# First conv of a graph-network kernel by three half-rate products, with its weight sums and the blend moved in the opening

## The chip, the cores and the metric

One NeuronCore of a Trainium2 chip runs the whole kernel. The metric is the device time of one execution in microseconds (us). The engines are named as in the profile: PE is TensorE, DVE is VectorE, ACT is ScalarE, POOL is GpSimd, SP only starts DMAs.

## What is computed

For 64 graphs of 128 nodes with 128 features, x and a 0/1 adjacency:

```
h = relu(layernorm(x))
c = relu(bn1(conv1(h)))                       # kernel width 1
x_conv = relu(bn2(conv2(c)) + h)              # width 17, padded by 8, along the nodes
s = h @ w_se.T + b_se                         # 3 coordinates
A = exp(-|s_n - s_m|^2) * adj
x_nmp = A @ relu(h @ w_msg.T + b_msg)
GRU gates r, z, n from [x_conv, x_nmp] and h; y = (1-z)*n + z*h
x = x + y
x = x + adj @ (relu(layernorm(x)) @ weight) + bias
```

## The kernel before

The graphs are worked on in 16 groups of four, and the groups in pairs: one pair (eight graphs) is a conv pass. `opening()` on every engine handles the first pair and prepares the second; then `step(t)`, t = 1 to 7 (the last without a front), runs the conv of pair t, the gates of that pair, the second layer of the pair before it and the front (norm, conv1, messages, distances) of the pair after. There is no scheduler: each engine's program is written out by hand, and semaphores (`have`, `wait_ge`, `then_inc`) tie the engines together. An engine works strictly in its written order.

Every product of 32-bit operands is split: each operand is rounded to a short part (`_hi`, by ACT's copy) and a rest (`_lo`, by DVE's subtraction), and `split_product` does three matmuls, hi x hi, hi x lo, lo x hi, of 512 or 256 columns.

The width-17 conv holds the nodes in four phases (node index modulo 4), `c1[:, 0:4]`. From `step(1)` on it is done by nine products of a quarter of the length over sums and differences of phases (`px`, made by `pre` on POOL) and over sums of taps (`conv` parts `M12`, `M22`, `M21`). For the first pair the kernel before uses the plain form instead: `direct(tap)` for 17 taps, each into both banks, pQ for the even outputs and pP for the odd ones. It then needs no differences, and POOL forms the tap sums (`sum_phases`) for `step(1)` meanwhile.

Names that the change touches, by engine:

- PE: `direct`, `x_turn(g)` (transposes of normed rows into PSUM), `rows_turn`, `distances`, `neighbour_sums`, `messages`, `gates_h`, `gates_n`, `gates_c`, `o_turn` (turns the blended output back), `keep_clock` (matmuls without use).
- ACT: `round_w(k)` rounds part k of the conv weights, `split_hi` and `split_hi_phases` round conv inputs to `cx_hi`, `conv1_out` writes `c1`, `first(g)` applies the norm, `hidden(g)` writes h, `left_rows`, `decay` (exp), `conv_round`, and the gates' tanh.
- DVE: `split_w(k)`, `split_lo` (`cx_lo`), `normalise1` (statistics), `shift1` (`nb`), `conv_out`, `conv_lo_out` (`xc_lo`), `sums_lo` (`n_lo`), `blend_start` and `blend_end` (the GRU blend), `residual`.
- POOL: `scale1` (the power -1/2 of the variance, `rs`), `pre`, `sum_phases`.

`f_done[i]` tell ACT and DVE that a conv product is complete. In the opening `f_done[3]` releases `conv_out(0, 0)` and `f_done[4]` releases `conv_out(0, 1)`. `residual(0)` follows the blend of group 0, and `messages(5)` is the messages product of group 5, in the front of `step(1)`.

## Time and profile before

| | us |
|---|---|
| median of three runs | 346.11 |
| lowest and highest | 343.37, 346.34 |
| the profiled execution, its own time | 344.95 |
| its span in the profile | 342.6 |
| TensorE busy in the span | 329.8 |
| VectorE busy | 261.6 |
| ScalarE busy | 220.5 |
| GpSimd busy | 152.1 |

The mean granted clock of TensorE was 0.995 of full speed. The profile shows one execution. The span runs from the first to the last instruction; the profiled execution's own time is 2.35 us longer, for what lies around it. In a timeline a row gives start, duration, engine, line, operation and tiles, and in brackets how long the engine had been idle before and what ended that. A matmul's duration includes filling and draining the array, so that matmuls in a row overlap; what each costs is the distance between two starts.

### The profile page before, as it was taken

To read this page: it belongs to the slowest core of one execution; us is meant where nothing else is said; L and a number is where in the kernel's file an instruction comes from. 1 tells how busy PE (TensorE), PEld (TensorE's weight loads), DVE (VectorE), ACT (ScalarE), POOL (GpSimd) and SP (SyncE) were. 2 spreads that over 40 slices of the span, in tenths; PEclk is the share of its full clock that TensorE was granted. 3 is DMA by queue.
4 is the path that set the end of the run, shared out by engine and by line. 5 is a ranking of instruction groups with operands and counts; after the bars stand their busy time and mean duration, and the time that the engine had idled before them with its cause. 6 is when DMAs were issued, how large, how long until landed. Compare 5 with 4: busy or idle time off the path is not lost.

```text
span 342.6 us, 6310 instructions
## 1 busy us (share of the span) xinstructions
PE 329.8 (96%) x2198; PEld 296.3 (86%) x2198; DVE 261.6 (76%) x735; ACT 220.5 (64%) x431; POOL 152.1 (44%) x131
## 2 busy tenths in 40 slices
PE   7699979999999999999999999999999999999995
PEld 5489958799988999899988999889988998899894
DVE  5576896899688995899688995899687895784474
ACT  2938835876865876676865876676866763444353
POOL 7053271024952189024952189024950189029014
PEclk9989999999999999999999999999999999999999
DMA  7900020001220022001210023001100000000003
GB/s 234 340 5 0 6 89 0 2 1 33 92 64 0 2 83 76 29 0 33 94 62 0 2 71 114 2 0 33 64 32 2 0 33 31 2 1 2 0 1 123
DMA packets 7951, 15.02 MB, mean 44 GB/s; under 512 B 1008, under 2 KB 1648, under 8 KB 7792
## 3 DMA queue, kind: packets, MB, share of 16 engines
q1 hardware_dynamic: 7776, 14.62, 12.7%
q8 instruction: 17, 0.28, 0.4%
q14 instruction: 14, 0.11, 0.1%
q10 hardware_dynamic: 144, 0.01, 0.0%
HBM read 10.43 MB, written 4.19 MB: 43 GB/s over the span
## 4 chain that ended last, share of the span: by engine, by line
PE 65%; DVE 19%; ACT 9%; issue 4%; POOL 1%; DMA 1%; POOLq 0%; DVEq 0%; ACTq 0%
PE pQ L311 4%; PE pQ L312 4%; PE pQ L313 4%; PE pNR L311 4%; PE pNR L313 4%; PE pNR L312 4%; PE pF L424 4%; PE pP L311 4%; PE pP L312 4%; PE pP L313 4%; DVE st L981 3%; ACT work L750 2%; PE pZ L484 2%; PE pI L313 2%; PE pI L311 2%
## 5 line engine op out<-in xcount | busy, mean ns | idle before, releaser
L1331 POOL TENSOR_TENSOR rs<-ve,neg_half 128x4 f32<-128x4 f32 x15 | 15.6, 1040 | 90.6 <-DVE ve L1111 90.6
L1326 POOL TENSOR_TENSOR rs<-ve,neg_half 128x8 f32<-128x8 f32 (+1 forms) x9 | 15.5, 1721 | 73.1 <-DVE ve L988 73.1
L311 PE MATMUL pP<-cx_hi,conv_hi 128*128 128x256 f32 x154 | 45.0, 292 | 0.0
L313 PE MATMUL pP<-cx_hi,conv_lo 128*128 128x256 f32 x154 | 43.5, 282 | 0.0
L312 PE MATMUL pP<-cx_lo,conv_hi 128*128 128x256 f32 x154 | 43.3, 281 | 0.0
L311 PE MATMUL pQ<-cx_hi,conv_hi 128*128 128x256 f32 x126 | 37.0, 293 | 0.0
L750 ACT ACTIVATE work<-work,nb,rs 128x128 f32<-128x128 f32 x60 | 24.8, 483 | 17.5 <-DVE nb L1115 17.0
L312 PE MATMUL pQ<-cx_lo,conv_hi 128*128 128x256 f32 x126 | 35.4, 281 | 0.0
L313 PE MATMUL pQ<-cx_hi,conv_lo 128*128 128x256 f32 x126 | 35.3, 281 | 0.0
L311 PEld LDWEIGHTS pP<-cx_hi,conv_hi 128*128 128x128 f32 x154 | 29.1, 189 | 0.3
L312 PEld LDWEIGHTS pP<-cx_lo,conv_hi 128*128 128x128 f32 x154 | 29.1, 189 | 0.3
L313 PEld LDWEIGHTS pP<-cx_hi,conv_lo 128*128 128x128 f32 x154 | 29.0, 188 | 0.0
L1069 DVE TENSOR_TENSOR cx_lo<-px,cx_hi 128x576 fp32r<-128x576 f32 x28 | 27.2, 1008 | 0.8 <-ACT cx_hi L664 0.8
L312 PEld LDWEIGHTS pQ<-cx_lo,conv_hi 128*128 128x128 f32 x126 | 23.8, 189 | 0.3
L311 PEld LDWEIGHTS pQ<-cx_hi,conv_hi 128*128 128x128 f32 x126 | 23.8, 189 | 0.0
L313 PEld LDWEIGHTS pQ<-cx_hi,conv_lo 128*128 128x128 f32 x126 | 23.7, 188 | 0.0
L770 ACT ACTIVATE work<-pNR,rz_b 128x512 f32<-128x512 f32 x16 | 11.0, 689 | 19.5 <-PE pNR L313 19.0
L683 ACT ACTIVATE hn<-x_ring,nb,rs 128x128 f32<-128x128 f32 x56 | 22.5, 485 | 0.0
L1379 POOL TENSOR_TENSOR x_ring<-work,late 128x512 f32<-128x512 f32 x16 | 20.5, 1284 | 0.3 <-DVE nb L1279 0.3
L664 ACT ACTIVATE cx_hi<-px 128x576 fp32r<-128x576 f32 x28 | 17.6, 674 | 3.5 <-POOL px L966 3.1
L399 PEld LDWEIGHTS pNR<-early,hn 128*128 128x128 f32 x128 | 16.3, 189 | 3.0 <-issue 2.1
L779 ACT ACTIVATE work<-work,vec 128x512 f32<-128x512 f32 x16 | 11.6, 724 | 11.2 <-DVE work L1083 11.2
(287 smaller groups left out, 1058.0 us busy)
## 6 DMA issues: line engine op xcount, KB each, us to landing
x_ring<-x_in SPq DMA_DIRECT2D x16, 256.0 KB, 2.8
adj_ring<-adj_in SPq DMA_DIRECT2D x16, 256.0 KB, 3.0
out<-x_ring SPq DMA_DIRECT2D x15, 256.0 KB, 2.0
work<-conv_in SPq DMA_DIRECT2D x1, 1088.0 KB, 7.6
x_ring<-gate_in SPq DMA_DIRECT2D x1, 576.0 KB, 7.7
out<-x_ring SPq DMA_DIRECT2D x2, 128.0 KB, 1.8
early<-early_in SPq DMA_DIRECT2D x1, 129.5 KB, 4.5
late<-late_in SPq DMA_DIRECT2D x1, 128.0 KB, 7.9
```

The lines of the kernel that those rows point to most:

```text
L311: pe.matmul(acc, w_hi, m_hi, start=start, stop=False)
L312: pe.matmul(acc, w_hi, m_lo, start=False, stop=False)
L313: return pe.matmul(acc, w_lo, m_hi, start=False, stop=stop)
L399: last = pe.matmul(ms[:, j, 0:MS], graph(hn[g % 2], j), w_ms, start=False, stop=True, skip_group_check=True)
L424: last = pe.matmul(lane(sums_bank(g)[:], j), graph(msg[g % 2], j), graph(att[g % 2], j), start=True, stop=True)
L664: act.activation(cx_hi[:, CX_PARTS[k][0]:CX_PARTS[k][1]], cx_source(k), ACT.Copy).then_inc(cxhi_set, 1)
L683: last = act.activation(graph(hn[g % 2], j), xs(g, j), ACT.Identity, bias=nb1[:, i:i + 1], scale=rs1[:, i:i + 1])
L750: last = act.activation(graph(h2[g % 2], j), graph(x1[g % 2], j), ACT.Relu, bias=nb2[g % 2][:, j:j + 1], scale=rs2[g % 2][:, j:j + 1])
L1069: dve.tensor_tensor(cx_lo[:, part], cx_source(k), cx_hi[:, part].bitcast(F32), ALU.subtract)\
L1326: pool.tensor_tensor(rs1[:, lane], ve1[:, lane], neg_half[:, lane], ALU.pow).then_inc(rs1_set, 1)
L1331: pool.tensor_tensor(rs2[g % 2][:], ve2[g % 2][:], neg_half[:, 0:GG], ALU.pow).then_inc(rs2_set, 1)
L1379: pool.tensor_tensor(xs(g).rearrange("p (g d) -> p g d", g=GG), x1[g % 2].rearrange("p (g d) -> p g d", g=GG), l1_bias, ALU.add).then_inc( ...
```

## The change

The first conv of the first eight graphs is done by three series of eight taps at half rate, and tap 16 by itself. With even and odd phases E and O of the input and even and odd taps, pQ collects even taps times (E - O), pP first collects (even + odd taps) times O. VectorE adds that sum, scaled, to both `base` tiles (`with_sum`), which frees pP for odd taps times (next E - O). VectorE makes both differences (`less_odd`, `next_less_odd`) and takes over the tap sums from GpSimd: `sum_odd` (M21 and M23) at the start, `sum_halves` (M12, M22) behind the first `conv_lo_out`. The conv weights are rounded in seven parts in another order, and four conv inputs of 576 elements are split in place of two. Statistics of groups 4 and 5 move behind the second `conv_lo_out` and ahead of the blend; GpSimd's `pre` 4 and 5 go behind `scale1([4, 5])`. `x_turn(4)` on TensorE goes behind `o_turn(0)`. The orders on ScalarE and VectorE are rewritten to fit, and `blend_end(0)` is moved ahead of the splits for `step(1)`. From `step(1)` on the programs are the same but for the counts that are waited for.

```diff
-        W_PARTS = (taps(8, A0), taps(8, A2), taps(1, T16), taps(4, M22), taps(8, M12), taps(8, M21))
-        W_SUMS = (0, 0, 0, 2, 2, 3)
+        W_PARTS = (taps(4, A0), taps(4, A2), taps(1, T16), taps(8, M21), None, taps(4, M22), taps(8, M12))
+        W_SUMS = (0, 0, 0, 1, 0, 3, 2)
...
+        def w_part(w, k):
+            if k == 4:
+                return w[:, taps(16, A0)].rearrange("p (a b w) -> p b a w", a=2, b=2)[:, 1]
+            return w[:, W_PARTS[k]]
...
+        FIRST_FILLS = (None, 3, 4, 0, 4)
...
+        FIRST_AT = (X11, X32, X12, X13)
+
+        def first_source(k):
+            return (px[:, 0:2], c1[:, 2:4], c1[:, 0:2], px[:, 2:4])[k]
+
+        def first_place(t, k):
+            return t[:, FIRST_AT[k]:FIRST_AT[k] + 2]
...
-            def direct(tap, start=False, stop=False):
...
+            def half_rate(bank, part, w, j, start=False, stop=False):
                 w_hi, w_lo = conv_hi[:, w * D:(w + 1) * D], conv_lo[:, w * D:(w + 1) * D]
+                x = FIRST_AT[part]
+                if j % 2 == 0:
+                    parts = [(bank[:], slice(x, x + 2), j // 2)]
+                else:
+                    parts = [(bank[:, 0:CG * QN], slice(x + 1, x + 2), j // 2),
+                             (bank[:, CG * QN:], slice(x, x + 1), j // 2 + 1)]
+                for acc, phases, at in parts:
+                    last = split_product(acc, w_hi, w_lo, cx_hi[:, phases, :, at * GG:at * GG + QW],
+                                         cx_lo[:, phases, :, at * GG:at * GG + QW], start, stop)
+                return last
+
+            def even_tap(j):
+                return half_rate(pQ, 0, (A0, A2)[j % 2] + j // 2, j, start=j == 0)
+
+            def sum_tap(j):
+                return half_rate(pP, 1, (M21, M23)[j % 2] + j // 2, j, start=j == 0, stop=j == 6)
+
+            def odd_tap(j):
+                return half_rate(pP, 3, (A1, A3)[j % 2] + j // 2, j, start=j == 0)
...
                 messages(0)
                 keep_clock(6)
                 pe.wait_ge(w_split, 1)
+                pe.wait_ge(cxlo_set, 1)
+                even_tap(0)
+                even_tap(2)
+                even_tap(4)
+                even_tap(6)
+                messages(1)
+                pe.wait_ge(w_split, 2)
+                even_tap(1)
+                even_tap(3)
+                even_tap(5)
+                even_tap(7).then_inc(f_done[0], 1)
+                pe.wait_ge(w_split, 4)
                 pe.wait_ge(cxlo_set, 2)
-                direct(0, start=True)
-                direct(4)
-                direct(8)
-                messages(1)
-                direct(12)
-                direct(1)
-                direct(5)
+                sum_tap(0)
                 rows_turn(0)
-                direct(9)
+                sum_tap(2)
                 x_turn(2)
-                direct(13)
+                sum_tap(4)
                 rows_turn(1)
+                sum_tap(1)
                 distances(0)
-                pe.wait_ge(w_split, 2)
-                direct(2)
+                sum_tap(3)
                 conv1(2)
+                x_turn(3)
+                sum_tap(5)
                 distances(1)
                 messages(2)
-                x_turn(3)
-                direct(6)
+                sum_tap(7)
                 neighbour_sums(0)
-                direct(10)
+                sum_tap(6).then_inc(f_done[1], 1)
+                pe.wait_ge(cxlo_set, 3)
+                half_rate(pQ, 2, T16, 8, stop=True).then_inc(f_done[3], 1)
                 conv1(3)
                 neighbour_sums(1)
-                direct(14)
                 messages(3)
+                pe.wait_ge(w_split, 5)
+                pe.wait_ge(cxlo_set, 4)
+                pe.wait_ge(t0_set, 2)
+                odd_tap(0)
+                odd_tap(2)
                 rows_turn(2)
-                direct(3)
+                odd_tap(4)
+                odd_tap(6)
+                rows_turn(3)
                 distances(2)
-                direct(7)
-                rows_turn(3)
-                direct(11)
+                odd_tap(1)
                 distances(3)
+                odd_tap(3)
                 neighbour_sums(2)
-                direct(15)
-                pe.wait_ge(w_split, 3)
-                even, odd = direct(16, stop=True)
-                even[2].then_inc(f_done[3], 1)
-                odd[0].then_inc(f_done[0], 1)
-                odd[1].then_inc(f_done[1], 1)
-                odd[2].then_inc(f_done[4], 1)
+                odd_tap(5)
+                odd_tap(7)
+                half_rate(pP, 1, T16, 8, stop=True).then_inc(f_done[4], 1)
                 gates_h(0)
                 neighbour_sums(3)
                 gates_n(0)
                 gates_c(0)
                 gates_h(1)
-                x_turn(4)
                 gates_n(1)
                 o_turn(0)
+                x_turn(4)
                 gates_c(1)
...
+            def split_hi_first(k):
+                if k in (0, 3):
+                    act.wait_ge(diff_set, 2 if k else 1)
+                else:
+                    act.wait_ge(c1_set, 2)
+                act.activation(first_place(cx_hi, k), first_source(k), ACT.Copy).then_inc(cxhi_set, 1)
...
                 conv1_out(0)
-                hidden_graphs(1)
+                conv1_out(1)
                 act.wait_ge(conv_loaded, 16)
                 round_w(0)
-                conv1_out(1)
-                split_hi_phases(0)
-                split_hi_phases(1)
+                split_hi_first(0)
+                hidden_graphs(1)
                 round_w(1)
-                round_w(2)
                 messages(0)
                 place_bias(1)
+                split_hi_first(1)
+                round_w(2)
+                round_w(3)
+                split_hi_first(2)
                 residual_phases(0)
-                messages(1)
-                place_bias(2)
                 residual_phases(1)
                 act.wait_ge(gate_loaded, 16)
                 act.activation(gate_hi[:], gate, ACT.Copy).then_inc(gate_rounded, 1)
                 first(2)
+                messages(1)
+                place_bias(2)
+                hidden_rows(2)
+                first(3)
                 left_rows(0)
-                hidden(2)
-                first(3)
+                hidden_graphs(2)
...
                 conv_round(0, 0)
+                round_w(5)
+                conv_round(0, 1)
                 hidden_gate(0)
-                conv_round(0, 1)
-                first(4)
                 sums_hi(3)
+                round_w(6)
+                split_hi(1, 1)
                 reset_gate(0)
                 update_gate(0)
                 candidate(0)
-                split_hi(1, 1)
+                first(4)
                 split_hi(1, 2)
                 hidden_gate(1)
+                split_hi(1, 3)
+                split_hi(1, 4)
                 hidden(4)
                 first(5)
...
+            def less_odd():
+                dve.wait_ge(c1_set, 2)
+                dve.tensor_tensor(px[:, 0:2], c1[:, 0:2], c1[:, 2:4], ALU.subtract).then_inc(diff_set, 1)
+
+            def next_less_odd():
+                dve.tensor_tensor(px[:, 2:3], c1[:, 1:2], c1[:, 2:3], ALU.subtract)
+                dve.tensor_tensor(px[:, 3:4, :, 0:QR - GG], c1[:, 0:1, :, GG:QR], c1[:, 3:4, :, 0:QR - GG], ALU.subtract)\
+                   .then_inc(diff_set, 1)
+
+            def sum_odd():
+                dve.wait_ge(conv_loaded, 16)
+                two_by_two = conv[:, taps(16, A0)].rearrange("p (a b w) -> p a b w", a=2, b=2)
+                dve.tensor_tensor(conv[:, taps(8, M21)].rearrange("p (a w) -> p a w", a=2), two_by_two[:, :, 0],
+                                  two_by_two[:, :, 1], ALU.add).then_inc(wsum_set, 1)
+
+            def sum_halves():
+                dve.tensor_tensor(conv[:, taps(8, M12)], conv[:, taps(8, A0)], conv[:, taps(8, A2)], ALU.add)\
+                   .then_inc(wsum_set, 1)
+                dve.wait_ge(wsum_set, 2)
+                dve.tensor_tensor(conv[:, taps(4, M22)], conv[:, taps(4, M12)], conv[:, taps(4, M32)], ALU.add)\
+                   .then_inc(wsum_set, 1)
+
+            def with_sum(e):
+                dve.wait_ge(f_done[1], 1)
+                dve.wait_ge((sumE_set, sumO_set)[e], 1)
+                dve.scalar_tensor_tensor(base[e][:], phases(1), bn_a[:, 1:2], base[e][:], ALU.mult, ALU.add).then_inc(t0_set, 1)
...
                 have(dve, (sumE_set, sumO_set)[e], t + 1)
+                have(dve, t0_set, 0 if t else e + 1)
...
+                sum_odd()
+                less_odd()
                 split_w(0)
-                split_lo_phases(0)
-                split_lo_phases(1)
+                split_lo_first(0)
                 coordinates(0)
                 split_w(1)
                 normalise1([2, 3])
                 split_w(2)
+                split_w(3)
+                coordinates(1)
+                split_lo_first(1)
+                shift1([2, 3])
                 pair_rows(0)
-                coordinates(1)
-                shift1([2, 3])
...
+                with_sum(0)
+                with_sum(1)
+                split_lo_first(3)
...
                 masked(3)
+                conv_out(0, 0)
                 sums_lo(2)
-                conv_out(0, 0)
-                shift1([4, 5])
                 split_lo(1, 0)
                 conv_lo_out(0, 0)
+                sum_halves()
                 conv_out(0, 1)
-                split_lo(1, 3)
                 conv_lo_out(0, 1)
+                normalise1([4, 5])
                 sums_lo(3)
-                split_lo(1, 4)
+                split_w(5)
+                shift1([4, 5])
                 blend_start(0)
+                blend_end(0)
+                split_w(6)
                 split_lo(1, 1)
                 split_lo(1, 2)
-                blend_end(0)
+                split_lo(1, 3)
+                split_lo(1, 4)
                 hidden_lo(4)
...
-            def sum_phases():
...
             def opening():
-                pool.wait_ge(cxlo_set, 2)
                 scale1([2, 3])
-                sum_phases()
-                pre(pool, 1, 1)
-                pre(pool, 1, 2)
                 pool.wait_ge(pair_set, 4)
-                for k in range(3, 6):
+                for k in range(1, 4):
                     pre(pool, 1, k)
                 scale1([4, 5])
+                for k in range(4, 6):
+                    pre(pool, 1, k)
```

VectorE, from the `cx_lo` that stands between `conv_out(0, 1)` and the second `xc_lo`, before the change (the `work` rows are the blend of group 0, `h_lo` is `hidden_lo(4)`):

```order
L1069 TENSOR_TENSOR cx_lo<-px,cx_hi 128x576
L1130 SCALAR_TENSOR_TENSOR xc_lo<-pP,xc_hi 128x512
L1059 TENSOR_TENSOR n_lo<-pF,n_hi 128x512
L1069 TENSOR_TENSOR cx_lo<-px,cx_hi 128x576
L1080 SCALAR_TENSOR_TENSOR work<-work 128x512
L1083 TENSOR_TENSOR work<-pI,work 128x512
L1086 SCALAR_TENSOR_TENSOR work<-work,hT 128x512
L1069 TENSOR_TENSOR cx_lo<-px,cx_hi 128x576 x2
L1090 SCALAR_TENSOR_TENSOR work<-work 128x512
L1092 TENSOR_TENSOR work<-work 128x512
L1008 SCALAR_TENSOR_TENSOR h_lo<-pF,h_hi 128x512
L1098 SCALAR_TENSOR_TENSOR work<-pH,x_ring 128x512
```

and after it, from the statistics of groups 4 and 5 (`conv_lo` are `split_w(5)` and `split_w(6)`, `nb` the shift of groups 4 and 5):

```order
L1020 BN_STATS st<-x_ring 128x6 x8
L1024 BN_AGGR mv<-st 128x2 x8
L1027 TENSOR_SCALAR ve<-mv 128x8
L1098 TENSOR_TENSOR n_lo<-pF,n_hi 128x512
L1140 TENSOR_TENSOR conv_lo<-work,conv_hi 128x512
L1033 SCALAR_TENSOR_TENSOR nb<-mv,rs 128x8
L1145 SCALAR_TENSOR_TENSOR work<-work 128x512
L1148 TENSOR_TENSOR work<-pI,work 128x512
L1151 SCALAR_TENSOR_TENSOR work<-work,hT 128x512
L1155 SCALAR_TENSOR_TENSOR work<-work 128x512
L1157 TENSOR_TENSOR work<-work 128x512
L1140 TENSOR_TENSOR conv_lo<-work,conv_hi 128x1024
```

The statistics, the shift and two weight splits now stand in this place, and the four `cx_lo` that stood among these rows come behind them.

GpSimd behind `sum_phases`' second sum, before (`px` and `ac` are `pre` 1 to 5, `rs` is `scale1`):

```order
L1372 TENSOR_TENSOR work<-work 128x1024
L958 TENSOR_TENSOR px<-c 128x576
L961 TENSOR_TENSOR px<-c 128x4x140
L964 TENSOR_TENSOR ac<-c 128x576
L966 TENSOR_TENSOR px<-ac,px 128x576
L968 TENSOR_TENSOR px<-ac,px 128x4x140
L1326 TENSOR_TENSOR rs<-ve,neg_half 128x8 x2
```

and after, from `scale1([2, 3])` on:

```order
L1403 TENSOR_TENSOR rs<-ve,neg_half 128x8
L997 TENSOR_TENSOR px<-c 128x576
L1000 TENSOR_TENSOR px<-c 128x4x140
L1003 TENSOR_TENSOR ac<-c 128x576
L1403 TENSOR_TENSOR rs<-ve,neg_half 128x8
L1005 TENSOR_TENSOR px<-ac,px 128x576
L1007 TENSOR_TENSOR px<-ac,px 128x4x140
```

The three sums are gone (the last of them is the first row of the upper list), and the power of groups 4 and 5 stands between `pre` 3 and `pre` 4.

TensorE around the turn of group 4 (`pF<-ident,hn`) and the turn of the output of group 0 (`pH<-ident,work`), before:

```order
L381 MATMUL pF<-ident,hn 128x128 x4
L311 MATMUL pNR<-n_hi,gate_hi 128x512
L312 MATMUL pNR<-n_lo,gate_hi 128x512
L313 MATMUL pNR<-n_hi,gate_lo 128x512
L311 MATMUL pQ<-n_hi,gate_hi 128x512
L312 MATMUL pQ<-n_lo,gate_hi 128x512
L313 MATMUL pQ<-n_hi,gate_lo 128x512
L311 MATMUL pI<-n_hi,gate_hi 128x512
L312 MATMUL pI<-n_lo,gate_hi 128x512
L313 MATMUL pI<-n_hi,gate_lo 128x512
L474 MATMUL pH<-ident,work 128x128 x4
```

and after, from the z part of `gates_n(1)`:

```order
L326 MATMUL pQ<-n_hi,gate_hi 128x512
L327 MATMUL pQ<-n_lo,gate_hi 128x512
L328 MATMUL pQ<-n_hi,gate_lo 128x512
L326 MATMUL pI<-n_hi,gate_hi 128x512
L327 MATMUL pI<-n_lo,gate_hi 128x512
L328 MATMUL pI<-n_hi,gate_lo 128x512
L494 MATMUL pH<-ident,work 128x128 x4
L400 MATMUL pF<-ident,hn 128x128 x4
L326 MATMUL pNR<-xc_hi,gate_hi 128x512
L327 MATMUL pNR<-xc_lo,gate_hi 128x512
```

The turn of group 4 stood ahead of `gates_n(1)` and now stands behind `o_turn(0)`, ahead of `gates_c(1)`.

## Rows read from the trace of the kernel before

**Rows 1.** Busy time of each engine by stretches of the span, with the granted clock.

```profile
core 0: us, PE busy (x) PEld busy (x) DVE busy (x) ACT busy (x) POOL busy (x), PEclk, DMA share, GB/s
...
18.30:21.60 3.30, 3.30 (x9) 2.57 (x8) 3.09 (x24) 0.46 (x1) 0.98 (x1) 0.50 0.02 5
...
44.12:54.36 10.24, 7.71 (x46) 6.32 (x45) 8.35 (x33) 4.21 (x9) 6.93 (x5) 1.00 0.15 48
54.36:69.40 15.04, 14.65 (x71) 11.84 (x70) 11.97 (x25) 11.78 (x23) 0.00 (x0) 1.00 0.00 1
...
100.00:340.00 240.00, 238.28 (x1624) 216.79 (x1622) 185.39 (x510) 154.27 (x303) 108.59 (x82) 1.00 0.09 30
```

**Rows 2.** Timeline of TensorE: start, duration, engine, line, operation, tiles, idle before.

```profile
16.87 0.47 PE L337 MATMUL pQ<-cx_hi,conv_hi 128*128 128x512 f32 x1 [2.13 <-DVE cx_lo L1063]
...
18.34 0.63 PE L337 MATMUL pQ<-cx_hi,conv_hi 128*128 128x512 f32 x1
...
24.27 0.39 PE L337 MATMUL pP<-cx_hi,conv_hi 128*128 128x512 f32 x1
...
24.96 0.40 PE L337 MATMUL pQ<-cx_hi,conv_hi 128*128 128x512 f32 x1
...
50.35 0.50 PE L415 MATMUL pH<-right,left 128*128 128x512 f32 x1 [2.00 <-ACT left L737]
...
50.69 1.05 PE L424 MATMUL pF<-att,msg 128*128 128x128 f32 x8
...
54.39 0.40 PE L311 MATMUL pNR<-h_hi,gate_hi 128*128 128x512 f32 x1
...
69.44 0.28 PE L311 MATMUL pP<-cx_hi,conv_hi 128*128 128x256 f32 x1
...
76.42 1.13 PE L399 MATMUL pNR<-early,hn 128*128 128x131 f32 x8
```

**Rows 3.** Groups of instructions by line and shape, 0 to 69.4 us: busy and mean ns.

```profile
L337 PE MATMUL pQ<-cx_hi,conv_hi 128*128 128x256 f32 x16 | 5.0, 313 | 0.0
...
L337 PE MATMUL pQ<-cx_hi,conv_hi 128*128 128x512 f32 x9 | 4.3, 483 | 2.1 <-DVE cx_lo L1063 2.1
...
L1069 DVE TENSOR_TENSOR cx_lo<-px,cx_hi 128x576 fp32r<-128x576 f32 x4 | 2.9, 752 | 0.8 <-ACT cx_hi L664 0.8
```

**Rows 4.** Timeline of ScalarE.

```profile
12.80 1.08 ACT L676 ACTIVATE conv_hi<-work 128x1024 fp32r<-128x1024 f32 x1
...
57.20 1.64 ACT L683 ACTIVATE hn<-x_ring,nb,rs 128x128 f32<-128x128 f32 x4
```

**Rows 5.** Timeline of VectorE.

```profile
13.92 1.22 DVE L1074 TENSOR_TENSOR conv_lo<-work,conv_hi 128x1024 fp32r<-128x1024 f32 x1 [2.42 <-ACT conv_hi L676]
...
48.52 1.65 DVE L981 BATCH_NORM_STATS2 st<-x_ring 128x6 f32<-128x128 f32 x8
...
50.88 0.17 DVE L988 TENSOR_SCALAR ve<-mv 128x8 f32<-128x8 f32 x1
...
67.53 0.69 DVE L1098 SCALAR_TENSOR_TENSOR work<-pH,x_ring 128x512 f32<-128x512 f32 x1 [0.24 <-PE pH L474]
...
73.50 0.69 DVE L1092 TENSOR_TENSOR work<-work 128x512 f32<-128x512 f32 x1
```

**Rows 6.** Timelines of VectorE and GpSimd where both are at work.

```profile
79.32 0.15 DVE L1115 SCALAR_TENSOR_TENSOR nb<-mv,rs 128x4 f32<-128x4 f32 x1
...
83.52 1.15 DVE L1115 SCALAR_TENSOR_TENSOR nb<-mv,rs 128x4 f32<-128x4 f32 x1
...
87.52 1.83 DVE L1069 TENSOR_TENSOR cx_lo<-px,cx_hi 128x576 fp32r<-128x576 f32 x1
...
48.02 1.40 POOL L966 TENSOR_TENSOR px<-ac,px 128x576 f32<-128x576 f32 x1
...
51.13 1.65 POOL L1326 TENSOR_TENSOR rs<-ve,neg_half 128x8 f32<-128x8 f32 x1 [0.37 <-DVE ve L988]
...
83.37 1.28 POOL L1379 TENSOR_TENSOR x_ring<-work,late 128x512 f32<-128x512 f32 x1
...
87.36 1.38 POOL L1387 TENSOR_TENSOR base<-base,s 128x512 f32<-128x512 f32 x1
```

116 lines of the change are left out of this document (44 added, 72 removed).

## The prediction

> **What bounds the kernel now.** I read the busy time by stretches first. From 100 to 340 us TensorE is busy 238.28 of 240.00 us at clock 1.00 [rows 1]: there the kernel is bound by TensorE, and the change alters nothing in it. What the change can give is the moment at which TensorE enters that steady run. So I looked for the last point in the opening where it waits: the stretch 44.12 to 54.36 has 7.71 us of TensorE in 10.24, the stretch 54.36 to 69.40 has 14.65 in 15.04, while VectorE has 8.35 and 11.97 in them [rows 1]. VectorE has only 1.9 and 3.1 us of air there. The timeline of TensorE then gives the posts: first product of the first conv at 16.87 behind an idle 2.13, a wait of 2.00 at 50.35 for `left`, `gates_h(0)` at 54.39, the first product of `step(1)` at 69.44, and `messages(5)` at 76.42, from where on it hardly waits [rows 2].
>
> **The change part by part.**
> 1. Fewer products. Each three-product unit of 512 columns takes 0.69 us (24.27 to 24.96) [rows 2]. Before, the first conv has 34 of them: on pQ 9 products of 512 and 16 of 256 for each of the three lines, so 9 + 8 = 17 units, and pP as many [rows 3]. After, there are three series of 8 and two for tap 16: 26. That is 8 x 0.70 = 5.6 us less, all on TensorE's path.
> 2. The start. Before, ScalarE rounds eight taps (1.08 us at 12.80) ahead of the second conv1 output [rows 4]. Now that output comes first, near 12.6, then the difference `less_odd` on VectorE, one rounding and one `cx_lo`, with 576 elements at 0.75 each on VectorE [rows 3]: 12.6 + 0.8 + 0.8 + 0.7 + 0.8 gives 15.8, about 1.0 us earlier than 16.87. `sum_odd` (1,024 elements; the same size takes 1.22 [rows 5]) lies in the air before the difference, since `conv_in` is there when ScalarE begins at 12.80.
> 3. The clock. After the idle 2.13 us, the granted clock is 0.50 from 18.30 to 21.60 [rows 1], and a product begun at 18.34 takes 0.63 in place of 0.39 [rows 2]; eight products advance by 0.43 instead of 0.23, 1.6 us in all. The idle time before the first product halves to 1.1 us, so I take the fall as gone: 1.6 us, and nothing as the other end.
> 4. The waits before the gates. TensorE is idle for 2.5 us from 44.12 to 54.36 (10.24 less 7.71 [rows 1]), 2.00 of it at 50.35 [rows 2]; that goes. New ones come, since the row turns and distances now stand closer together while `gate_hi`, `first(2)` and `first(3)` stand ahead of `left_rows(0)` on ScalarE: I get 0.6 before `rows_turn(1)`, 1.0 before `distances(0)`, 0.2 before `distances(3)`. Net 0.7 less.
>
> These four bring `gates_h(0)` from 54.39 to 54.4 - 5.6 - 1.0 - 1.6 - 0.7 = 45.5. Were that all, the kernel would gain 8.9 us.
>
> 5. What VectorE must now do before TensorE can use it. The changed order adds `sum_odd`, `less_odd`, `next_less_odd`, `with_sum` twice, `sum_halves` and two further cx_lo: 1.2 + 0.75 + 0.9 + 1.4 + 1.9 + 1.5 = 7.6 us by 1.22 for 1,024 and 0.75 for 576 elements [rows 3, 5]. Some 4.5 us of it lie in the stretch to 40 us, beside the products: `with_sum` must be done before the odd taps, and by my count it is (35.5, with `cx_lo` at 36.2; TensorE gets there at 37). The rest lies behind. I follow VectorE from the third group's `neighbour_sums`, whose end goes from 51.6 (50.69 and 0.9 [rows 2]) to 45.5 - 3 x 0.7 = 43.4, since three units still follow it:
>    - n_hi on ScalarE and n_lo: 44.7. cx_lo of 288 elements 0.45, xc_lo 0.65: 45.8. `sum_halves` 1.9: 47.7. Second conv output 0.65, a wait of 0.7 for ScalarE's rounding (it stands behind `round_w(5)`), xc_lo 0.65: 49.7.
>    - The norm of groups 4 and 5 is here now. It is 48.52 to 51.05 in the old trace [rows 5], 2.5 us, where it filled a wait for the fourth `exp`. Now it stands ahead of the blend: 52.2. n_lo and `split_w(5)` 1.25: 53.4. GpSimd's power takes 1.65 [rows 6] and is done at 53.9.
>    - The port. Behind that power GpSimd now runs `pre` 4 and 5, 1.40 each [rows 6]. On VectorE the shift of 8 elements follows, then the first blend operation, both with two inputs from SBUF. Such an instruction waits until GpSimd's ends: the shift takes 0.15 at 79.32 and 1.15 at 83.52, when GpSimd's 83.37 + 1.28 ends at 84.65; and the cx_lo at 87.52 takes 1.83 for 0.75, until past 88.74 [rows 6]. So: shift 55.3, `pre` 5 to 56.7, first blend operation 57.3. That is 2.6 us more than the same work without GpSimd beside it. Bounds: 0 if it had slipped between, 2.8 if both are waited out in full; the rows speak for the upper end.
>    - The rest of the blend (0.69 an operation [rows 5], one ScalarE tanh between): v 58.0, oT 60.2. `split_w(6)` 1.15: 61.4. Four cx_lo 2.7: 64.1. ScalarE meanwhile (0.5 to 0.7 an operation of 512 or 576 elements): tanh to 58.7, `first(4)` 1.55 (1.64 at 57.20 [rows 4]), then two more cx_hi ahead of `hidden(4)` than before: done at 64.2. h_lo to 64.9, and `residual(0)` starts there, where it was 67.53 [rows 5]. That is 2.6 us earlier.
>
>    The Trainium skill says of this port, in "GPSIMD Engine Reference", section Specifications, that GpSimd's SBUF interfaces are shared with VectorE and that they contend when a VectorE instruction has two SBUF inputs or runs in a two-port mode. This trace agrees (1.15 against 0.15 us), and it speaks against the place of `pre` 4 and 5: by it the gain is 2.6 us, without it 5.2 us.
>
> 6. The moved turn. With x_turn(4) ahead of `gates_n(1)`, as before, TensorE would stand for `first(4)`, which ScalarE now does after the tanh. Behind `o_turn(0)` it costs nothing of its own. TensorE: 45.5 and 14 units of 0.70 and one `neighbour_sums` of 0.9 give 56.2; it waits 1.8 for v, does a unit, waits 1.4 for oT, does two turns of 0.45 and the three units of `gates_c(1)`, enters `step(1)` at 63.2 (6.2 us earlier than 69.44), waits 0.8 for `first(5)` and then again at `o_turn(1)`: oT of group 1 follows `residual(0)` by 6.7 us (67.53 to 73.50 + 0.69 [rows 5]), now 71.6, while TensorE is there at 69.8. So `messages(5)`, 8.9 us after `residual(0)` before (67.53 to 76.42 [rows 2, 5]), comes at 73.8 and not at 76.42. From there TensorE is the bound again and the order is the old one.
>
> **Sum.** Of 8.9 us at `gates_h(0)`, 6.2 are left at `step(1)` and 2.6 at `messages(5)`. The profiled execution took 344.95 us with a span of 342.6; 344.95 - 2.6 = 342.3. The median of the three runs before is 346.11, 1.2 above the profiled one, and their lowest 343.37; the sum goes by the profiled one, and the 1.2 only widens the range upwards.
>
> **The rivals.**
> - R1, no meeting on the port. If `pre` 4 and 5 or the shift fall so that VectorE is not held, 2.6 us more come back: 339.7. For it: VectorE could arrive later than GpSimd is done, if `round_w` or the waits before it run late. Against it: the shift is released by the very instruction that stands ahead of `pre` 4, so they start together.
> - R2, the clock falls in the new holes. TensorE is idle 1.8 and 1.4 us with 0.7 between, then 1.7 more at `o_turn(1)`; an idle 2.13 was followed by a clock of 0.50, an idle 2.00 at 50.35 was not [rows 1, 2]. A fall of the length seen costs 1.6 us; at 60 it is hidden by the later wait, at 73 it is not: 342.3 + 1.6 = 343.9.
> - R3, slower. The same holes, but the clock stays at 0.50, because VectorE's late steps of `step(1)` (oT, h_lo, bias) keep making small ones. Each us at half clock costs 0.5 us of products. The wait at `o_turn(1)`, 1.7, and the gain, 2.6, are used up after 8.6 us; past that the kernel is slower. A fall over 16 us, from 60 to 76, gives 344.95 - 2.6 + (8.0 - 1.7) = 348.6. Against it: it lasted 3.3 us in this trace.
> - R4, nothing arrives. If the holes before `left_rows(0)` and the late `with_sum` are each a us worse than counted, or VectorE meets GpSimd's `pre` 1 to 3 too, 2.5 us go: 344.9.
>
> **How the numbers follow.** The forecast has 0.48 with its own range 341.0 to 343.8; R1 0.22; R2 0.12; R4 0.10; R3 0.08. About 1% (3.5 us) is what a measurement of this kernel can tell from no change. Faster by over 1%: R1 and a fifth of the forecast and its neighbours, 0.38. Slower by over 1%: R3, 0.09. Within: 0.53. The range: low end just below R1 for the case that the port costs nothing and the start gives a bit more, 338.9; high end past R4 and the level of the median, 346.0.
>
> **What would show it.** Right: first conv product near 15.8; no clock of 0.50 near 19; `gates_h(0)` at 45 to 46; the blend's first two VectorE instructions above 1 us each beside GpSimd's px; `residual(0)` at 64 to 66; `messages(5)` some 2.6 us earlier. Wrong in point 3 if the clock still falls near 18; in point 4 if TensorE waits over 3 us before 45; in point 5 if the shift and the first blend operation take 0.2 and 0.7; in point 6 if TensorE enters `step(1)` and does not wait there. The forecast as a whole is wrong if `step(1)` of the new kernel is bound by something other than VectorE's blend.

## The result and the profile after

The changed kernel takes 340.76 us (median of 5 runs, 340.13 to 341.73); the kernel before, beside it, 344.80 (5 runs, 343.37 to 346.34). The ratio is 0.9862, interval 0.9825 to 0.9898: 1.4% faster, 4.0 us, where 2.6 were forecast. The profiled execution took 340.39 us with a span of 338.6 (before: 344.95 and 342.6).

The shares of the page first: engine, busy time, share, instructions.

```profile
PE 324.5 (96%) x2162; PEld 290.6 (86%) x2162; DVE 265.0 (78%) x746; ACT 221.5 (65%) x434; POOL 145.1 (43%) x128
```

Then the stretches that answer to [rows 1].

```profile
core 0: us, PE busy (x) PEld busy (x) DVE busy (x) ACT busy (x) POOL busy (x), PEclk, DMA share, GB/s
18.30:21.60 3.30, 3.30 (x27) 3.16 (x26) 3.23 (x16) 3.30 (x5) 1.67 (x1) 1.00 0.03 7
44.12:54.36 10.24, 10.24 (x54) 8.68 (x54) 8.72 (x28) 5.96 (x10) 1.77 (x2) 1.00 0.00 0
50.00:60.00 10.00, 8.21 (x37) 6.12 (x36) 9.31 (x27) 6.21 (x12) 4.89 (x3) 1.00 0.00 0
60.00:70.00 10.00, 8.75 (x60) 7.50 (x58) 9.67 (x29) 8.17 (x17) 2.02 (x1) 1.00 0.00 1
70.00:80.00 10.00, 9.02 (x67) 8.16 (x68) 9.39 (x47) 7.48 (x16) 2.49 (x3) 1.00 0.05 10
100.00:336.00 236.00, 234.28 (x1605) 213.78 (x1603) 181.87 (x504) 151.53 (x299) 108.54 (x82) 1.00 0.09 30
```

The clock near 19 is 1.00 where it was 0.50. TensorE's idle time from 44 to 54 is gone, but new idle time has come at 50 to 60 (1.79 us), 60 to 70 (1.25) and 70 to 80 (0.98), and there VectorE is busy 9.31, 9.67 and 9.39 of 10 us: it has become the engine that TensorE waits for. From 100 on nothing has changed (TensorE is busy 234.28 of 236.00 us, 99.3%, as before). TensorE's timeline shows the posts, against [rows 2]:

```profile
16.14 0.48 PE L326 MATMUL pQ<-cx_hi,conv_hi 128*128 128x512 f32 x1 [1.03 <-DVE cx_lo L1102]
...
27.69 0.50 PE L435 MATMUL pZ<-right,left 128*128 128x512 f32 x1 [1.30 <-ACT left L771]
...
41.80 0.47 PE L435 MATMUL pH<-right,left 128*128 128x512 f32 x1 [0.28 <-DVE right L1085]
...
45.82 0.39 PE L326 MATMUL pNR<-h_hi,gate_hi 128*128 128x512 f32 x1
...
57.02 0.49 PE L326 MATMUL pI<-n_hi,gate_hi 128*128 128x512 f32 x1 [0.36 <-DVE work L1148]
...
59.41 0.75 PE L494 MATMUL pH<-ident,work 128*128 128x128 f32 x4 [1.43 <-DVE work L1157]
...
62.52 0.28 PE L326 MATMUL pP<-cx_hi,conv_hi 128*128 128x256 f32 x1
...
70.38 0.75 PE L494 MATMUL pI<-ident,work 128*128 128x128 f32 x4 [1.51 <-DVE work L1157]
...
72.55 1.13 PE L418 MATMUL pNR<-early,hn 128*128 128x131 f32 x8 [0.46 <-ACT pNR L757]
```

`gates_h(0)` starts 8.57 us earlier (45.82, before 54.39), `step(1)` 6.92 (62.52, before 69.44), `messages(5)` 3.87 (72.55, before 76.42). All the waits behind 45.82 but the last name VectorE. VectorE in that stretch, against [rows 5]:

```profile
46.11 1.22 DVE L1121 TENSOR_TENSOR work<-work 128x1024 f32<-128x1024 f32 x1
...
49.99 1.63 DVE L1020 BATCH_NORM_STATS2 st<-x_ring 128x6 f32<-128x128 f32 x8
...
53.02 0.68 DVE L1140 TENSOR_TENSOR conv_lo<-work,conv_hi 128x512 fp32r<-128x512 f32 x1
...
54.25 1.38 DVE L1033 SCALAR_TENSOR_TENSOR nb<-mv,rs 128x8 f32<-128x8 f32 x1 [0.56 <-POOL rs L1403]
...
55.56 0.68 DVE L1145 SCALAR_TENSOR_TENSOR work<-work 128x512 f32<-128x512 f32 x1
...
56.88 1.15 DVE L1151 SCALAR_TENSOR_TENSOR work<-work,hT 128x512 f32<-128x512 f32 x1
...
63.68 0.68 DVE L1165 SCALAR_TENSOR_TENSOR work<-pH,x_ring 128x512 f32<-128x512 f32 x1
...
69.64 0.69 DVE L1157 TENSOR_TENSOR work<-work 128x512 f32<-128x512 f32 x1
```

And GpSimd beside it, against [rows 6]:

```profile
52.59 1.64 POOL L1403 TENSOR_TENSOR rs<-ve,neg_half 128x8 f32<-128x8 f32 x1 [8.87 <-DVE ve L1027]
...
54.19 1.43 POOL L1005 TENSOR_TENSOR px<-ac,px 128x576 f32<-128x576 f32 x1
...
55.57 1.90 POOL L1007 TENSOR_TENSOR px<-ac,px 128x560 f32<-128x560 f32 x1
```

ScalarE's tanh in the middle of the blend:

```profile
57.00 0.73 ACT L813 ACTIVATE work<-work,vec 128x512 f32<-128x512 f32 x1 [3.11 <-DVE work L1148]
```

The shift of 8 elements, released by the power that ends at 54.23, is held until `pre` 4 ends and takes 1.38 us. The first blend operation at 55.56 is not held (0.68): this time GpSimd's `pre` 5, begun at 55.57, is the one that is longer, 1.90 us for the 1.43 of its neighbour. The third blend operation meets what is left of it (1.15 for 0.68). `residual(0)` starts at 63.68, and `messages(5)` follows it by 8.87 us, as it did before (8.89).

### The profile page after: what moved, and what is told of

Same layout as the page of the kernel before. It is cut to its first block, busy times and chain, and to the rows that moved or that the text cites. A ratio compares the mean times of both kernels' runs of the same rounds, so it can differ in the third digit from the quotient of the medians.

```text
span 338.6 us, 6261 instructions
## 1 busy us (share of the span) xinstructions
PE 324.5 (96%) x2162; PEld 290.6 (86%) x2162; DVE 265.0 (78%) x746; ACT 221.5 (65%) x434; POOL 145.1 (43%) x128
## 4 chain that ended last, share of the span: by engine, by line
PE 62%; DVE 17%; ACT 8%; issue 7%; POOL 3%; DMA 1%; POOLq 0%; DVEq 0%; ACTq 0%
PE pQ L326 5%; PE pQ L328 5%; PE pQ L327 5%; PE pP L328 4%; PE pP L326 4%; PE pP L327 4%; PE pNR L326 4%; PE pNR L327 4%; PE pNR L328 4%; PE pF L444 3%; DVE st L1020 2%; ACT work L784 2%; PE pZ L504 2%; PE pI L326 2%; PE pI L328 2%
## 5 line engine op out<-in xcount | busy, mean ns | idle before, releaser
L326 PE MATMUL pP<-cx_hi,conv_hi 128*128 128x256 f32 (+1 forms) x179 | 53.8, 301 | 0.0
L328 PE MATMUL pP<-cx_hi,conv_lo 128*128 128x256 f32 (+1 forms) x179 | 51.6, 288 | 0.0
L327 PE MATMUL pP<-cx_lo,conv_hi 128*128 128x256 f32 (+1 forms) x179 | 51.4, 287 | 0.0
L326 PE MATMUL pQ<-cx_hi,conv_hi 128*128 128x256 f32 (+1 forms) x139 | 41.5, 299 | 1.0 <-DVE cx_lo L1102 1.0
L327 PE MATMUL pQ<-cx_lo,conv_hi 128*128 128x256 f32 (+1 forms) x139 | 39.7, 286 | 0.0
L328 PE MATMUL pQ<-cx_hi,conv_lo 128*128 128x256 f32 (+1 forms) x139 | 39.7, 285 | 0.0
L326 PEld LDWEIGHTS pP<-cx_hi,conv_hi 128*128 128x128 f32 x179 | 33.9, 190 | 0.6
L327 PEld LDWEIGHTS pP<-cx_lo,conv_hi 128*128 128x128 f32 x179 | 33.9, 189 | 0.5
L328 PEld LDWEIGHTS pP<-cx_hi,conv_lo 128*128 128x128 f32 x179 | 33.7, 188 | 0.4
L997 POOL TENSOR_TENSOR px<-c 128x576 f32<-128x576 f32 x7 | 10.0, 1435 | 18.4 <-DVE pair L1078 18.4
```

The lines of the kernel that those rows point to most:

```text
L326: pe.matmul(acc, w_hi, m_hi, start=start, stop=False)
L327: pe.matmul(acc, w_hi, m_lo, start=False, stop=False)
L328: return pe.matmul(acc, w_lo, m_hi, start=False, stop=stop)
```

## The experiments

The kernels ran in three groups. Those of one group ran on the same chip and share the runs of the kernel before, whose median is 345.97 us in the first group (15 runs), 344.79 in the second (10), 344.60 in the third (13). The first group are the four that take from TensorE, give to VectorE, or move work on GpSimd; the second are the repeated kernel, the blend ahead of the shift, the norm and the turn; the third are the last four, on the clock. The changed kernel itself ran only beside the result (340.76) and in the second group (340.82). Times of different groups are compared directly below; for it speaks that the kernel before, in its runs at a mean clock of 1.00, took 342.8 to 343.5 us in all three groups. Unless another is named, each edit is made on the changed kernel.

### The changed kernel again

No edit.

> The changed kernel once more, unedited, as the measure for the three others of its group. 340.8 us within 0.8, about 4 us under the kernel before; TensorE comes to the messages of graph 5 at 72.5 within 0.3, at a granted clock of 1.00.

340.82 us (340.20 to 341.70, 4 runs), ratio 0.989 (0.9853 to 0.9928). The time repeats and every post up to 72 us is 0.2 earlier, but the clock did not do what was expected: behind the same wait the granted clock is 0.73 in this profile, and the products of `messages(5)` take 2.08 us in place of 1.13. The stretches behind the wait (the granted clock is the third number from the end, 0.73 and 0.89):

```profile
70.00:74.00 4.00, 3.31 (x14) 2.71 (x15) 3.41 (x21) 2.96 (x6) 0.23 (x1) 0.73 0.01 4
74.00:80.00 6.00, 6.00 (x48) 5.96 (x47) 5.00 (x25) 4.12 (x10) 1.48 (x2) 0.89 0.00 0
```

TensorE's timeline there:

```profile
72.36 2.08 PE L418 MATMUL pNR<-early,hn 128*128 128x131 f32 x8 [0.48 <-ACT pNR L757]
```

So one program shows both, with spans of 338.6 and 339.5. Single profiles of it may not be compared to within 1 us behind 72.

### Where VectorE's chain is the bound: less for TensorE, more for VectorE

```
 odd_tap(1); distances(3); odd_tap(3); neighbour_sums(2)
-odd_tap(5)
-odd_tap(7)
```

> The changed kernel without odd taps 5 and 7 (two units of three products, 1.4 us of TensorE, are left out of the first conv). Theory V: gates_h(0) starts 1.4 us earlier, near 44.4, but residual(0) and messages(5) move by less than 0.3, and the time is that of the changed kernel, 0.986 of the kernel before. Rival T: all posts and the time go 1.4 us down, 0.982.

340.57 us (340.26 to 341.21, 4 runs), ratio 0.988 (0.9825 to 0.9934). `gates_h(0)` comes at 44.21, 1.61 earlier, and `messages(5)` at 72.37, 0.18 earlier; 0.2 of both is there from the first product on, as in the repeated kernel, beside which `residual(0)` (63.49) and `messages(5)` (72.36) do not move at all. The clock also falls in this profile, to 0.50 in 59 to 61, and the wait at 70.21 (0.80 for VectorE, 1.51 without the edit) hides that as well. TensorE's timeline:

```profile
44.21 0.40 PE L326 MATMUL pNR<-h_hi,gate_hi 128*128 128x512 f32 x1
...
72.37 1.13 PE L418 MATMUL pNR<-early,hn 128*128 128x131 f32 x8 [0.48 <-ACT pNR L755]
```

The second edit adds useless work on VectorE.

```
+for j in range(GG):
+    dve.bn_stats(st2[:, j, :], xs(2, j))
+dve.tensor_tensor(work[:, NW * D:], conv[:, taps(3, A0)], conv[:, taps(3, A2)], ALU.add)
 sum_halves()
```

> The changed kernel with some 1.3 us of work without use on VectorE ahead of sum_halves (four statistics of 128 elements and one sum of 384). Theory V: residual(0) and messages(5) come 1.3 us later, near 65.0 and 73.8, and 1.3 us are lost of the gain, 0.990 of the kernel before. Rival T: gates_h(0), messages(5) and the time move by less than 0.3 us.

341.63 us (341.11 to 343.07, 8 runs), ratio 0.9905 (0.9874 to 0.9937); 0.9 above the changed kernel by the medians, and 0.7 to 1.0 by the four runs at a clock of 1.00 (341.1 to 341.4, beside 340.4). `gates_h(0)` stays at 45.72, `residual(0)` is 1.12 later, `messages(5)` 1.13 later. TensorE's timeline:

```profile
73.68 2.09 PE L418 MATMUL pNR<-early,hn 128*128 128x131 f32 x8 [0.48 <-ACT pNR L757]
```

VectorE's:

```profile
64.80 0.68 DVE L1165 SCALAR_TENSOR_TENSOR work<-pH,x_ring 128x512 f32<-128x512 f32 x1
```

Take 1.4 us of products away and nearly nothing comes; give VectorE 1.3 us and nearly all of it arrives at the posts. That settles which engine bounds the stretch of 46 to 72 us.

### What the port costs: GpSimd's `pre` ahead of the power

```
 scale1([2, 3])
-for k in range(1, 4):
+for k in range(1, 6):
     pre(pool, 1, k)
 scale1([4, 5])
-for k in range(4, 6):
-    pre(pool, 1, k)
```

> The changed kernel with one edit on GpSimd: pre 4 and 5 run straight behind pre 3, and the power of groups 4 and 5 comes last. Theory P (the port): the shift of groups 4 and 5, which took 1.38 us beside pre 4, takes 0.15, and the third blend operation 0.69 in place of 1.15; residual(0) starts about 1.2 us earlier than 63.68, near 62.5, messages(5) near 71.4 in place of 72.55, and the kernel is 1.2 us faster than the changed one, near 0.983 of the kernel before. Rival (the meeting only moves): pre 4 or 5 then holds the cx_lo of 288 elements at 45.15 or the first weight sum at 46.1 for as long, and residual(0) stays within 0.3 of 63.68.

340.73 us (339.57 to 341.09, 4 runs), ratio 0.9872 (0.9824 to 0.992): no gain in the median. In the profile the price of the port at the shift is gone (0.17 for 1.38), but 0.6 of it has moved to the first weight sum, which now runs beside `pre` 5. VectorE's timeline:

```profile
46.22 1.82 DVE L1121 TENSOR_TENSOR work<-work 128x1024 f32<-128x1024 f32 x1
...
54.98 0.17 DVE L1033 SCALAR_TENSOR_TENSOR nb<-mv,rs 128x8 f32<-128x8 f32 x1 [0.56 <-POOL rs L1403]
...
63.16 0.68 DVE L1165 SCALAR_TENSOR_TENSOR work<-pH,x_ring 128x512 f32<-128x512 f32 x1
```

`residual(0)` is 0.52 earlier and `messages(5)` 0.51 (72.04); there its products take 1.76 us at a mean clock of 0.83 in 70 to 80. In this profile the half microsecond was won and lost again to the clock. The one run at a mean clock of 1.00 took 339.57, 0.8 under the changed kernel's 340.39; the other three, at 0.993 and 0.994, took 340.6 to 341.1.

### The weight sums on GpSimd

The two sums go from VectorE to GpSimd, ahead of `pre` 1, and all five `pre` ahead of the power.

```
 # VectorE
-sum_halves()
 # GpSimd
 pool.wait_ge(pair_set, 4)
+pool.wait_ge(wsum_set, 1); pool.tensor_tensor(conv[:, taps(8, M12)], ...)
+pool.wait_ge(wsum_set, 2); pool.tensor_tensor(conv[:, taps(4, M22)], ...)
-for k in range(1, 4):
+for k in range(1, 6):
     pre(pool, 1, k)
```

> The changed kernel with sum_halves on GpSimd, ahead of pre 1, and pre 1 to 5 ahead of the power. Theory V (VectorE's chain sets when step(1) runs freely): 1.9 us of sums and the port's 1.2 leave the chain; residual(0) near 60.5, messages(5) near 69.5, the kernel 3 us faster than the changed one, near 0.977 of the kernel before. Rival T (TensorE or ScalarE is only just behind VectorE): under 1 us, 0.983 or above.

338.36 us (337.96 to 339.13, 6 runs), ratio 0.9812 (0.9773 to 0.9851): 2.4 us under the changed kernel, and as much by the runs at a clock of 1.00 (338.0 beside 340.4). That is less than the 3 us expected. GpSimd takes 2.39 and 1.29 us for the sums that cost VectorE 1.22 and 0.69, but it has the time. `residual(0)` is 2.38 earlier and `messages(5)` (70.17) as much: 1.86 for the sums (46.11 to 47.97), 1.2 for the shift, 0.2 for the blend, less 0.8 for a cx_lo of 288 elements that is now held (1.24 for 0.45). VectorE's timeline:

```profile
45.07 1.24 DVE L1128 TENSOR_TENSOR cx_lo<-c,cx_hi 128x288 fp32r<-128x288 f32 x1
...
61.30 0.68 DVE L1158 SCALAR_TENSOR_TENSOR work<-pH,x_ring 128x512 f32<-128x512 f32 x1
```

GpSimd's `pre` 2, behind which that cx_lo was held:

```profile
44.59 1.41 POOL L1000 TENSOR_TENSOR px<-c 128x560 f32<-128x560 f32 x1
```

### The blend ahead of the shift

On top of the last one.

```
-shift1([4, 5])
 blend_start(0)
+shift1([4, 5])
 blend_end(0)
```

> On top of the version with the two weight sums on GpSimd: VectorE makes the first three operations of the blend of group 0 ahead of the shift of groups 4 and 5, so that they fill its wait of 0.57 us for GpSimd's power. If VectorE's chain still bounds this stretch: residual of group 0 at 60.7 (61.30 there), messages of graph 5 0.5 earlier, 337.9 against 338.4. If the bound there has gone over to ScalarE or TensorE: 338.4, and the residual at 61.3 or the wait ahead of the output turn of group 1 no shorter by place.

337.29 us (337.16 to 338.28, 4 runs), ratio 0.9796 (0.9754 to 0.9837). The wait of 0.57 us is filled; `residual(0)` starts at 60.55 and `messages(5)` at 69.43, 0.74 earlier, of which 0.14 was there at 45 us already (the cx_lo at 44.93, before 45.07). By the runs at 1.00 it is 0.8 faster (337.2 to 337.3, before 338.0). VectorE's chain is still the bound. VectorE's timeline:

```profile
54.32 0.16 DVE L1033 SCALAR_TENSOR_TENSOR nb<-mv,rs 128x8 f32<-128x8 f32 x1
...
60.55 0.68 DVE L1158 SCALAR_TENSOR_TENSOR work<-pH,x_ring 128x512 f32<-128x512 f32 x1
```

### The norm of groups 4 and 5 back in its old place

```
+normalise1([4, 5])
 masked(3)
 conv_out(0, 0)
+shift1([4, 5])
 sums_lo(2)
...
 conv_lo_out(0, 1)
-normalise1([4, 5])
 sums_lo(3)
 split_w(5)
-shift1([4, 5])
 blend_start(0)
```

> Undoes one part of the change: the norm of groups 4 and 5 goes back ahead of the mask of group 3, its shift right behind the first convolution output. VectorE has the same work, but neither its wait of 0.56 us for GpSimd's power nor the shift held to 1.38 us. If VectorE's sum bounds the stretch: second convolution split 2.4 later (51.8), TensorE waits about 1.6 for it, but residual of group 0 at 62.0 to 62.8 (63.68), messages of graph 5 about 1.2 earlier, 339.6. Rival, the late norm is what pays (TensorE's gates come late without it): residual at 64.5 or later and 341.5 to 342.5. No difference to the changed kernel within 0.4 would mean that order and wait trade off exactly.

342.44 us (341.65 to 342.98, 7 runs), ratio 0.9919 (0.9891 to 0.9948): 1.6 slower than the changed kernel in the same group, the rival's number (1.3 by the runs at a clock of 1.00: 341.7 beside 340.4); `messages(5)` is 1.5 later (73.88, there 72.36). VectorE's list of work is the same, but the second convolution's split is late, TensorE waits 2.18 for it, and the tanh that the blend needs is late in turn. VectorE then waits 0.88. Earlier it waits 0.46 for the power, and GpSimd holds it here too: the shift takes 1.36, behind `pre` 4, and the cx_lo of 288 elements 1.09 for 0.45. TensorE's timeline:

```profile
54.40 0.50 PE L326 MATMUL pNR<-xc_hi,gate_hi 128*128 128x512 f32 x1 [2.18 <-DVE xc_lo L1198]
```

VectorE's:

```profile
46.88 1.36 DVE L1033 SCALAR_TENSOR_TENSOR nb<-mv,rs 128x8 f32<-128x8 f32 x1 [0.46 <-POOL rs L1403]
...
56.89 0.69 DVE L1145 SCALAR_TENSOR_TENSOR work<-work 128x512 f32<-128x512 f32 x1 [0.88 <-ACT work L804]
...
65.00 0.68 DVE L1165 SCALAR_TENSOR_TENSOR work<-pH,x_ring 128x512 f32<-128x512 f32 x1
```

So the late norm is a part of the gain: what lies ahead of the blend is not only a sum of durations on VectorE, it also has to be in the order in which it is needed. My count for this run, `messages(5)` 1.2 earlier and 339.6 us, left out who needs what first, and its time was wrong by 2.8.

### The turn of group 4 back ahead of the gate products

```
 gates_h(1)
+x_turn(4)
 gates_n(1)
 o_turn(0)
-x_turn(4)
 gates_c(1)
```

> The turn of group 4 stands again ahead of the neighbour products of gate 1, as before the change. By my step 6 it then waits for ScalarE's rows of group 4 (written at 59.3 in the changed kernel) with 2.1 us of gate products queued behind it, so the output turn of group 0 is 2.1 to 2.3 us later than 59.4, and the wait of 1.51 us ahead of the output turn of group 1 takes most of that back: 0.5 us slower than the changed kernel (341.3), the messages of graph 5 at 73.1. Rival, the place of the turn is worth its full 2.1 us: 342.9. Rival, its place does not matter since VectorE bounds this stretch: 340.8. Rival, the hole of about 4 us ahead of the turn lets the clock fall: granted clock under 0.8 somewhere in 59 to 66 and 342.0 to 342.9.

341.23 us (340.64 to 342.13, 4 runs), ratio 0.9903 (0.9865 to 0.994), 0.4 above the changed kernel, which is less than the runs' spread. TensorE's timeline:

```profile
59.13 0.66 PE L400 MATMUL pF<-ident,hn 128*128 128x128 f32 x4 [4.05 <-ACT hn L716]
...
62.96 0.94 PE L494 MATMUL pH<-ident,work 128*128 128x128 f32 x4
...
72.89 1.13 PE L418 MATMUL pNR<-early,hn 128*128 128x131 f32 x8
```

TensorE stands for 4.05 us in one piece, the output turn of group 0 is 3.7 later, `residual(0)` waits 0.44 for it and `messages(5)` is 0.53 later than in the changed kernel of this group, which is what was expected. The clock falls (0.83 in 60 to 70), which the posts do not separate from the effect of the turn.

### The clock: the kernel before with its hole filled

```
 messages(0)
-keep_clock(6)
+keep_clock(13)
```

> The kernel before with thirteen useless 128-column products instead of six between the messages of graph 0 and the first convolution product, so that they fill 1.7 of the 2.13 us that TensorE waits there. It makes the changed kernel's clock at that place (my step 3) without its products. Theory: granted clock 1.00 in 18.3 to 21.6 and the products behind 1.6 us earlier, but the next wait for ScalarE and VectorE takes nearly all of it back: gates of graph 0 begin at 54.4 less at most 0.5, 344.3 to 344.8. Rival, the clock's 1.6 us arrive in full: 343.2. Rival, the clock falls for another reason (0.6 in 18.3 to 21.6 as before): 344.8.

344.42 us (342.85 to 344.79, 10 runs) beside 344.60 (342.83 to 346.34, 13 runs), ratio 0.9975 (0.9949 to 1.0001). In its profile (343.02 us, span 341.2) the clock stays at 1.00 and the rival's reading holds, the gain arrives in full: `gates_h(0)` at 53.05 and `messages(5)` at 75.08, both 1.34 earlier, although the first product starts 0.23 later. The stretch near 19:

```profile
18.30:21.60 3.30, 3.30 (x17) 2.68 (x16) 3.13 (x22) 0.69 (x2) 0.75 (x1) 1.00 0.02 5
```

TensorE's timeline:

```profile
17.10 0.47 PE L337 MATMUL pQ<-cx_hi,conv_hi 128*128 128x512 f32 x1 [0.57 <-DVE cx_lo L1063]
...
49.04 0.50 PE L415 MATMUL pH<-right,left 128*128 128x512 f32 x1 [2.00 <-ACT left L737]
...
53.05 0.40 PE L311 MATMUL pNR<-h_hi,gate_hi 128*128 128x512 f32 x1
```

The wait before the mask of group 2 is still 2.00 us (49.04, before 50.35). It took nothing back. ScalarE's `left` stands behind a rounding that waits for GpSimd's `pre` 4, and that chain came 1.3 earlier too (`pre` 4 at 46.71, before 48.02). ScalarE's timeline:

```profile
48.14 0.68 ACT L664 ACTIVATE cx_hi<-px 128x576 fp32r<-128x576 f32 x1 [3.06 <-POOL px L966]
```

The median shows little of it (0.2 us); the mean of the runs moves by 1.0 (343.9, beside 344.9). Beside the experiments the kernel before ran 38 times: 7 at a mean clock of 1.00 took 342.8 to 343.5 us, 15 at about 0.995 took 344.4 to 345.1, and 16 at 0.990 to 0.994 took 345.9 to 346.6. The filled one has 4 runs at 1.00 (342.9 to 343.1) and 6 at 0.995 (344.4 to 344.8), and none above. I read that as one of two falls gone, each worth 1.5 us. Where the other lies no profile here shows: of the fourteen profiles eight have one fall, and none has two.

### The clock: the changed kernel with its hole left open

```
 messages(0)
-keep_clock(6)
```

> The changed kernel without the six useless products ahead of the first convolution product, so that TensorE waits 2.5 us there instead of 1.03. Theory: granted clock about 0.6 in 18.3 to 21.6 as in the kernel before, the products behind it up to 1.6 us later, of which the wait of 1.30 us for ScalarE's left rows at 27.7 takes most back; gates of graph 0 at 45.8 to 46.3, 340.8 to 341.3. Rival, the clock costs its full 1.6 us: gates at 47.4 and 342.4. Rival, the clock stays at 1.00 there with a hole of 2.5 us: 340.8 and step 3 of my prediction had the wrong cause.

341.51 us (341.29 to 341.73, 4 runs), ratio 0.9894 (0.9863 to 0.9925), 0.7 above the unedited kernel of another group. The profile does not show what was expected: behind an idle 2.37 us the clock stays at 1.00. TensorE's timeline, and then the stretch near 19:

```profile
15.97 0.47 PE L326 MATMUL pQ<-cx_hi,conv_hi 128*128 128x512 f32 x1 [2.37 <-DVE cx_lo L1101]
```

```profile
18.30:21.60 3.30, 3.30 (x27) 3.17 (x27) 3.20 (x17) 3.30 (x5) 1.67 (x1) 1.00 0.01 2
```

It is longer than the 2.13 us that were followed by the fall in [rows 1, 2], so the hole's length alone does not decide. The fall came at 72 instead, as in the repeated kernel. The test is inconclusive on what brings a fall, and so is step 3 of the prediction on its cause: the new order has no fall near 19, but that the shorter wait is the reason is not shown.

### The clock: the last hole filled

```
 # TensorE, step(1)
+have(pe, v_set, 2)
+for _ in range(5):
+    pe.matmul(pI[:, 0:N], ident[:], ident[:], start=True, stop=True)
 o_turn(1)
```

> The changed kernel with five useless 128-column transposes' worth of products into the bank that the output turn of group 1 is about to fill, behind the sum that reads it: they fill 1.2 of the 1.51 us that TensorE waits at 70. Two profiles of the unedited changed kernel had a granted clock of 1.00 and of 0.80 behind this wait, at 338.6 and 339.5 us of span. If the wait is the cause of the fall: granted clock 1.00 in 70 to 80 in this profile, messages of graph 5 at 72.5 and 1.1 to 1.2 long, median 340.2 to 340.6 and a narrower spread. If not: the clock falls as often as before, 340.8.

340.21 us (339.95 to 340.40, 4 runs), ratio 0.9856 (0.9825 to 0.9887). The clock fell in this profile too, but at another place, behind the waits at 57 and 59, and `messages(5)` starts at 72.44 and takes 1.13. The stretches behind those waits:

```profile
59.00:61.00 2.00, 1.71 (x9) 1.71 (x9) 2.00 (x4) 2.00 (x5) 0.00 (x0) 0.57 0.00 0
61.00:63.00 2.00, 2.00 (x8) 1.60 (x7) 2.00 (x5) 2.00 (x5) 0.00 (x0) 0.58 0.00 0
```

TensorE was 0.9 us later at the messages of graph 4 (66.82, before the filler 65.95), and the hole ahead of the output turn of group 1 took all of it. Since the fall had already come, this profile does not show whether the filler keeps one away at 70. The nine runs of the changed kernel reach to 341.73; here none passes 340.40, which fits the expectation, but four runs are few.

The same filler on the best version:

> The version with the weight sums on GpSimd and the blend ahead of the shift (337.3 us), with the same filler ahead of the output turn of group 1. Its profile had no fall of the clock, so the filler should bring little: 337.0 to 337.3, clock 1.00 in 70 to 80. If the filler's products delay the output turn: messages of graph 5 later than 69.4 and 337.8 or more.

337.22 us (337.08 to 337.24, 4 runs), ratio 0.9769 (0.9733 to 0.9806), beside 337.29 (337.16 to 338.28) without it. This is the fastest kernel of the study, 3.6 us under the changed one; the wait at `o_turn(1)` reads 0.37 (before the filler 1.45) and nothing moves: the turn starts at 67.27 (67.25 without the filler) and `messages(5)` at 69.44 (69.43).

## Why the prediction was right, and which term was not

The sign and the mechanism were right: TensorE gains 8.6 us up to `gates_h(0)`, and VectorE's chain gives 4.7 of it back.

- Step 1, fewer products, and step 4, the waits. `gates_h(0)` was forecast at 45.5 and came at 45.82. The new waits before it are 1.30 and 0.28, 1.6 in all for 1.8 forecast; but 1.30 of it is in one place, ahead of `distances(0)`. What is left of the 8.57 us behind the start (0.7), the waits (0.95 net, 2.53 before and 1.58 now) and the clock (1.3 to 1.6) is 5.3 to 5.6, for the 5.6 of the missing products.
- Step 2, the start: 16.14 in the profile, 15.71 to 16.00 in the other profiles that have this order, 15.8 forecast (its terms add up to 15.7).
- Step 3, the clock: 1.00 near 19 in every profile of a kernel with the new order, so the fall is gone there. Why is open: the forecast put it down to the shorter wait, but the kernel without the useless products waits 2.37 and has 1.00 too, and 7 of 38 runs of the kernel before have no fall at all. It is worth 1.5 us, by the filled kernel before (1.34 at both posts of its profile, 1.5 between the levels of its runs).
- Step 5, VectorE's chain. The order of the chain was right and the experiments with less for TensorE and more for VectorE confirm it. Its one wrong term is the port: "first blend operation 57.3. That is 2.6 us more". Measured, the shift cost 1.2 more and the third operation at most 0.2 on the chain (it ends 0.3 behind ScalarE's tanh, at 57.73), 1.4 in all. The forecast had counted that VectorE loses each meeting, because it did in [rows 6]; here GpSimd lost the second. The Trainium skill says in "GPSIMD Engine Reference", section Specifications, that two SBUF inputs on VectorE contend with GpSimd; both meetings agree (1.38 for 0.17 on VectorE, 1.90 for 1.43 on GpSimd), but `split_w(5)` at 53.02 has two such inputs too and took its usual 0.68 beside the power. `residual(0)` was forecast at 64.9 and came at 63.68 (the power was 0.3 later than forecast, and h_lo came 0.3 sooner behind the cx_lo), and that 1.2 runs through unchanged: oT(1) 71.6 forecast, 69.64 + 0.69 measured; `messages(5)` 73.8 and 72.55.
- Step 6, the moved turn. TensorE waited 0.36 for v and not 1.8, since v was there at 56.96 (56.27 and 0.69; 58.0 forecast) and TensorE itself 0.5 later than forecast. It waited 1.43 for oT (1.4), nothing for `first(5)` (0.8 forecast) and 1.51 at `o_turn(1)` (1.7). The turn's place itself is worth 0.5 us by the profile of the run that undid it, where the clock fell as well.
- The sum. 342.3 forecast for an execution that took 344.95 before; 340.39 measured. Of the 1.9 between them 1.25 is the port, and 0.56 lies outside the spans, where no run explains it: 344.95 - 342.6 is 2.35 us, and 340.39 - 338.6 is 1.79.

Of the rivals, R1 (no meeting) was wrong as worded, since they met, but its 339.7 is nearer to the case of the profile than the forecast. R2 was real: in four profiles of kernels with this chain (the repeated one, the one with `pre` first, the one with more on VectorE, the unfilled one) the clock falls to 0.5 behind the wait at 70, and its price is 0.9 us between the two spans of the changed kernel, and 1.1 to 2.0 between the runs of the one with more on VectorE (341.1 to 341.4 at 1.00, 342.5 and 343.1 at 0.995): 1.6 was no bad figure. Its other half, that a fall at 60 is hidden, is borne out by the kernel with fewer products (`messages(5)` at 72.37). R3's lasting fall was never seen, R4's 2.5 us neither.

The median moved more than the schedule did. At a clock of 1.00 the kernel before takes 343.1 us (7 runs, 342.8 to 343.5) and the profiled run of the changed one 340.4, so the schedule is worth 2.7 us. That this is near the 2.6 forecast is luck: the forecast counts from an execution with the fall at 18 us, and by its own sum would give only 1.0 from one without. By the levels of the runs, the remaining 1.3 of the 4.0 are falls of the clock. The kernel before has them in 31 of 38 runs, at 1.5 us each. The changed one has them as often, in eight of its nine runs, but three of those eight took 340.1 to 340.4, no more than the one at 1.00: there, it seems, a wait hid the fall.

## What to carry to other kernels

Follow a gain from post to post to the last wait for another engine: of 8.6 us that TensorE gained at the first gates, 3.9 were left where it is the bound again, and the way to more of it was to take work off VectorE and fill its wait (a further 3.5 us); taking 1.4 us of products off TensorE moved no post of VectorE. When an operation of that chain is moved, ask who needs each of its neighbours first; equal sums in another order cost 1.6 us here. And before two kernels are compared by one profile each, look at the granted clock by stretches in both: one fall costs some 1.5 us where nothing hides it, and comes in some runs and not in others.

## What the runs showed of the hardware

- Two sides of the shared port. A VectorE instruction with two SBUF inputs that started behind a GpSimd sum of 560 or 576 elements was held until that ended (0.17 to 1.38, 0.45 to 1.24, 1.22 to 1.82 us). One that started 0.01 us ahead of it was not held, and the GpSimd instruction took 1.90 for 1.43; in the kernel with `pre` first, a cx_lo 0.03 ahead of `pre` 5 kept its 0.45 and `pre` 5 took 1.67 for 1.39. GpSimd's power of 8 elements held nothing, though it runs for 1.64 us: `split_w(5)`, in the middle of it, took 0.68 (53.02). The norm's statistics, one SBUF input, kept their time: 1.63 at 48.84 beside `pre` 5 in the kernel with the weight sums on GpSimd, 1.63 at 49.99 alone in the changed one.
- A fall of the granted clock is of one size wherever it came: in [rows 1] 3.3 us at 0.50 (TensorE's 1.2 GHz level, 1.00 being 2.4), 0.57 and 0.58 over the 4 us from 59 to 63 in the kernel with the filler. Eight of the fourteen profiles have one, at 18, 59 to 60 or 71 to 73 us. What it costs depends on what follows: 1.3 to 1.5 us at 18 us in the kernel before, where the chains of the other engines moved with TensorE; 0.9 to 2.0 at 72, where TensorE is the bound from there on; nothing at 59, since the wait at 70 takes it (`messages(5)` at 72.37 and 72.44 with a fall there, 72.36 in the repeated kernel, without one there).
- The same program's clock fell at 72 in one profile and not in another, and an idle 2.37 us was not followed by a fall where an idle 2.13 us had been. What decides it stays open.
